# Cross-attention queries projected in the first output projection's stage and read back from DRAM, with the weighting of the values one step later

## What is computed

```
x1 = x + attention(layernorm(x)) @ o_proj.T          # first output projection
n  = layernorm(x1)
q  = rope(rms_norm(n @ Wq.T))        # 16 heads of 128; a head's norm is over its 128 columns
k  = rope(rms_norm(concat(ctx, n) @ Wk.T))           # 4 key heads, each for 4 query heads
v  = concat(ctx, n) @ Wv.T
x2 = x1 + (softmax(q k.T / sqrt(128)) v) @ Wo.T      # second output projection
```

## Time and profile before

| | |
|---|---|
| time, median of 3 runs | 2584.07 us (2581.47 to 2589.3) |
| profiled execution, span from the first to the last instruction | 2582.5 us |
| span of the first output projection (571 to 779) | 208 us |
| cross-attention before its first score (779 to 857.3) | 78.3 us |
| cross-attention, 60 steps with projections (857.3 to 1964.75) | 1107.45 us |
| cross-attention, last 4 steps and store (1964.75 to 2034) | 69.25 us |
| mean granted TensorE clock | 0.940 of full |

### The profile page before, as it was taken

How to read it: one execution, slowest core, us unless ns; L and a number is a source line. 1 busy time by engine, 2 the same in 40 slices (tenths; PEclk the granted TensorE clock), 3 DMA queues, 4 the chain that set the end, 5 groups by cost and what they waited for, 6 DMA issues and landing times. The chain is left out here.

```text
span 2582.5 us, 35584 instructions
## 1 busy us (share of the span) xinstructions
PE 2250.8 (87%) x10576; PEld 1665.7 (64%) x10576; DVE 1444.7 (56%) x3200; ACT 1022.2 (40%) x1998; POOL 784.9 (30%) x832
## 2 busy tenths in 40 slices
PE   5689999968975999999999999999998698928991
PEld 3578888857754666666666666666664476727771
DVE  3535555558764556565656565665664455535554
ACT  2323333334223444444454445444444422115660
POOL 1400000004553333333333333332331012136664
PEclk8899999989997999999999999999999899959996
DMA  7521221127764101111111011111100443235335
GB/s 274 164 72 36 65 64 32 37 73 230 223 190 166 37 12 45 40 44 40 44 41 44 12 44 41 44 40 44 40 15 15 147 111 92 63 120 189 110 102 191
DMA packets 229859, 218.95 MB, mean 85 GB/s; under 512 B 113394, under 2 KB 191714, under 8 KB 227298
## 3 DMA queue, kind: packets, MB, share of 16 engines
q1 hardware_dynamic: 212770, 180.46, 22.3%
q0 software_dynamic: 6496, 18.37, 2.6%
q10 hardware_dynamic: 10464, 18.77, 2.1%
HBM read 136.72 MB, written 80.83 MB: 84 GB/s over the span
## 5 line engine op out<-in xcount | busy, mean ns | idle before, releaser
L1820 DVE TENSOR_REDUCE ca_top<-ca_ps_s 112x1 f32<-112x487 f32 x256 | 169.3, 661 | 353.7 <-PE ca_ps_s L1608 351.6
L1708 ACT ACTIVATE ca_prob<-ca_ps_s,ca_down,ca_q_scale 112x487 f32<-112x487 f32 x256 | 193.9, 758 | 194.9 <-DVE ca_down L1822 194.8
L1608 PE MATMUL ca_ps_s<-ca_kT,ca_qT 128*112 128x487 f32 x512 | 241.0, 572 | 0.8 <-ACT ca_kT L1694 0.8
L1523 POOL TENSOR_TENSOR ca_q_scale<-ca_ssum,ca_minus_half 112x4 f32<-112x4 f32 x64 | 64.5, 1007 | 571.4 <-DVE ca_ssum L1809 571.4
L1626 PE MATMUL ca_ps_o<-ca_pT,ca_v 125*128 125x448 f32 (+1 forms) x512 | 222.4, 559 | 2.5 <-ACT ca_pT L1715 2.5
L91 PE MATMUL out_ps_y<-out_w_hi,out_o_hi 128*128 128x512 f32 x448 | 185.1, 413 | 33.2 <-DVE out_o_lo L1174 32.8
L1615 PEld LDWEIGHTS ca_ps_t<-ca_ident,ca_prob 112*125 112x125 f32 x1024 | 140.7, 188 | 109.2 <-DVE ca_prob L1829 76.7
L91 PE MATMUL ca_ps_p<-ca_w_hi,ca_xh 128*112 128x512 f32 x384 | 184.1, 479 | 29.2 <-DMA ca_tab<-rope_tables 25.2
L1615 PE MATMUL ca_ps_t<-ca_ident,ca_prob 112*125 112x112 f32 x1024 | 164.8, 283 | 42.3 <-DVE ca_prob L1829 42.2
L93 PE MATMUL out_ps_y<-out_w_hi,out_o_lo 128*128 128x512 f32 x448 | 180.5, 403 | 0.0
L92 PE MATMUL out_ps_y<-out_w_lo,out_o_hi 128*128 128x512 f32 x448 | 180.3, 403 | 0.0
(11 more groups left out here) (271 smaller groups left out, 5457.8 us busy)
## 6 DMA issues: line engine op xcount, KB each, us to landing
self_outT<-sa_ov SPq DMA_DIRECT2D x64, 224.0 KB, 2.4
out_o_raw<-self_outT SPq DMA_DIRECT2D x56, 256.0 KB, 4.2
cross_outT<-ca_ov SPq DMA_DIRECT2D x64, 224.0 KB, 2.3
out_o_raw<-cross_outT SPq DMA_DIRECT2D x56, 256.0 KB, 3.3
ffn_raw<-in_expert_w SPq DMA_DIRECT2D x8, 1536.0 KB
ca_c_raw<-in_ctxT SPq DMA_DIRECT2D x16, 750.0 KB, 6.4
expert_rows<-ffn_yt ACTq DMA_DIRECT2D x42, 256.0 KB, 2.0
rope_tables<-out_tab SPq DMA_DIRECT2D x16, 640.0 KB, 4.2
```

The costliest lines, as they stand in the source:

```text
L1608: pe.matmul(ps_s[j % 2][:, :], qT[:, i, j, :], kT[par][:, i, :], start=True, stop=True).then_inc(scored.sem, 1)
L1708: act.activation(prob[j][:, 0:KV], ps_s[j % 2][:, :], ACT.Exp, bias=down[:, j:j + 1], scale=q_scale[par][:, i, j:j + 1], accum_out=total[: ...
L1820: dve.tensor_reduce(top[:, j:j + 1], ps_s[j % 2][:, :], AX.X, ALU.max, negate=True).then_inc(maxed.sem, 1)
```

## The change

The queries leave the cross-attention. `self_output` takes the place of `project_out` in the first output stage, keeps all of its work and does more in each tile: it projects the queries of the tile it has just turned (`query`, four units of 12 matmuls), ACT squares them, DVE multiplies them with a table and sums the squares (`rotate`), POOL adds, roots and scales them (`unit`), PE turns them (`turn_q`), ACT copies them (`keep`) and SP stores them in DRAM as `cross_qT`. 14 tiles of 128 rows take the place of 16 sequences of 112 rows. The query weights (4 MB) are loaded and split here, their `lo` parts by POOL. The raw loads share memory with the `lo` parts (`both`), so a chunk of the next tile is loaded only when PE has used this one (`used`). The guest's `angles`, `sine` and `make` work on 128 x 320 elements, for the tables of the 128-row tile.

The cross-attention loads one 224 KB piece of `cross_qT` in each step, splits two weights and not six, and its `step` has another order: `weigh` of the step before stands behind the first two scores, the two projections follow, and DVE's sums of squares are set apart from `rotate`. The scale and the `down` product are gone. `cross_output` is the old `project_out` with its router branch alone.

```diff
+            def rotate(t, i, par):
...
+                if i == 0:
+                    wait(dve, guest.made, t)
+                wait(dve, q_sq, t, i)
+                wait(dve, q_turned, t, i - 2)
+                dve.tensor_tensor(h4(r1), h4(ps), over_heads(tab[:, 4, 0, :], HQ), ALU.mult)
+                for half in range(2):
+                    this, other = slice(half * HF, (half + 1) * HF), slice((1 - half) * HF, (2 - half) * HF)
+                    ins = dve.tensor_tensor(h4(r2)[:, :, this], h4(ps)[:, :, other],
+                                            over_heads(tab[:, 4, 1, this], HQ), ALU.mult)
+                ins.then_inc(q_rot.sem, 1)
+                wait(dve, q_rooted, t, i - 2)
+                dve.tensor_reduce(sm, h4(sq[i % 2][:, :]), AX.X, ALU.add).then_inc(q_sum.sem, 1)
+                wait(dve, q_sum, t, 2 * i)
+                f = 1.0 / X_SCALE ** 2
+                dve.tensor_scalar(sm, sm, f / HD, RMS_EPS * f, ALU.mult, ALU.add).then_inc(q_sum.sem, 1)
...
+            def body(t, h, par, ahead=True, last=False):
+                turn(t, par)
+                if ahead:
+                    low(t + 2, 0)
+                    low(t + 2, 1)
+                if not last:
+                    add(t + 1, h + par, 1 - par)
+                rotate(t, 0, par)
+                if not last:
+                    scale(t + 1, 1 - par)
+                if ahead:
+                    low(t + 2, 2)
+                rotate(t, 1, par)
+                if ahead:
+                    low(t + 2, 3)
+                guest.angles(dve, t + 2, par)
+                rotate(t, 2, par)
+                rotate(t, 3, par)
...
+            def unit(t, i):
+                a, b, par = q1[i % 2][:, :], q2[i % 2][:, :], i % 2
+                wait(pool, q_rot, t, i)
+                pool.tensor_tensor(a, a, b, ALU.add).then_inc(q_added.sem, 1)
+                wait(pool, q_sum, t, 2 * i + 1)
+                pool.tensor_tensor(rstd[par][:, :], ssum[par][:, :], minus_half[:, :], ALU.pow).then_inc(q_rooted.sem, 1)
+                wait(pool, q_rooted, t, i)
+                wait(pool, q_added, t, i)
+                heads = a.rearrange("p (h d) -> p h d", h=HQ)
+                pool.tensor_tensor(heads, heads, along(rstd[par][:, :], HD), ALU.mult).then_inc(q_ready.sem, 1)
...
+            def body(t, h, par, last=False):
+                if not last:
+                    layer.root(pool, t + 1, minus_half)
+                for i in range(NQ):
+                    unit(t, i)
+                guest.make(pool, t + 2, h + 1, par)
...
+            def body(t, h, par, ahead=True, first=False):
+                if not first:
+                    keep(t - 1, 2)
+                    keep(t - 1, 3)
+                turn(t, h, par)
+                if ahead:
+                    high(t + 2, 0)
+                    high(t + 2, 1)
+                square(t, 0)
+                if ahead:
+                    high(t + 2, 2)
+                square(t, 1)
+                if ahead:
+                    high(t + 2, 3)
+                guest.sine(act, t + 2, par)
+                square(t, 2)
+                keep(t, 0)
+                square(t, 3)
+                keep(t, 1)
...
+            def query(t, i, par):
...
+                wait(pe, q_rot, t, i - 2)
...
+            def turn_q(t, i):
+                wait(pe, q_ready, t, i)
+                wait(pe, q_kept, t, i - 2)
...
+            def body(t, par, first=False, last=False):
+                if not last:
+                    project(t + 1, 1 - par, 0)
+                if not first:
+                    turn_q(t - 1, 2)
+                if not last:
+                    project(t + 1, 1 - par, 1)
+                if not first:
+                    turn_q(t - 1, 3)
+                turn(t, par)
+                if not last:
+                    project(t + 1, 1 - par, 2)
+                    project(t + 1, 1 - par, 3)
+                query(t, 0, par)
+                query(t, 1, par)
+                query(t, 2, par)
+                turn_q(t, 0)
+                query(t, 3, par)
+                turn_q(t, 1)
```

The order of the new query work on ACT, DVE, PE and POOL is that of the four `body` functions above. In the cross-attention PE's and DVE's lists change so:

```diff
+            def step(b, h, i, par, more):
+                score(b, h, i, 0, par)
+                score(b, h, i, 1, par)
+                if begun(b, i):
+                    pb, pi = before(b, i)
+                    weigh(pb, pi, par if i else 1 - par)
                 if more:
-                    project(b + 1, i, 0, 1 - par)
+                    keys(b + 1, h + par, i, 1 - par)
                 turn(b, i, 0)
-                score(b, i, 2, par)
                 turn(b, i, 1)
-                score(b, i, 3, par)
+                score(b, h, i, 2, par)
+                score(b, h, i, 3, par)
                 if more:
-                    project(b + 1, i, 1, 1 - par)
-                    turn_q(b + 1, i)
+                    values(b + 1, i, 1 - par)
                 turn(b, i, 2)
                 turn(b, i, 3)
                 if more:
-                    project(b + 1, i, 2, 1 - par)
-                weigh(b, i, par, (0, 1))
-                if more:
                     turn_k(b + 1, i)
-                weigh(b, i, par, (2, 3))
 
             batches(pe, start, step)
+            weigh(B - 1, 3, 1)
...
+            def step(b, h, i, par, more):
+                maximum(b, i, 0)
+                maximum(b, i, 1)
                 divide(b, i, 0)
                 divide(b, i, 1)
                 if more:
-                    rotate(b + 1, i, 0, 1 - par)
-                maximum(b, i, 2, par)
-                maximum(b, i, 3, par)
+                    rotate(b + 1, h + par, i, 1 - par)
+                maximum(b, i, 2)
+                maximum(b, i, 3)
+                if more:
+                    squares(b + 1, i)
                 divide(b, i, 2)
                 divide(b, i, 3)
-                if more:
-                    rotate(b + 1, i, 1, 1 - par)
-
```

More of the change, by code:

```diff
@@ new lines, in _ @@
+            for h in range(H):
+                sp.dma_start(w_raw[:, h, :], w_src[:, h, :]).then_inc(w_in[h // HQ], 16)
+                if h % HQ == 0:
+                    load(0, h // HQ)
+                if h == 0:
+                    guest.load(sp)
+            residual(0, 0)
+            residual(1, 1)
+            for c in range(NQ):
+                sp.dma_start(wq_raw[:, c, :, :], wq_src[:, :, c * D:(c + 1) * D]).then_inc(wq_in[c], 16)
+                load(1, c)
+            body(0, 0, 0, first=True)
@@ new lines, in _ @@
+            body(1, 0, 1)
+            with sp.Fori(1, TT // 2 - 1) as h:
+                for par in range(2):
+                    body(h * 2 + par, h, par)
+            for par in range(2):
+                body(TT - 2 + par, TT // 2 - 1, par, ahead=False)
+            store_q(TT - 1, 2)
+            store_q(TT - 1, 3)
+            for par in range(2):
+                guest.store(sp, TT + par, par)
+            for par in range(2):
+                sp.wait_ge(guest.put[par].sem, guest.put[par].at(B // 2 - 1))
+                sp.wait_ge(y_put[par].sem, y_put[par].at(TT // 2 - 1))
+                sp.wait_ge(x_put[par].sem, x_put[par].at(TT // 2 - 1, 1))
+                sp.wait_ge(q_put[par].sem, q_put[par].at(TT - 1, 1))
@@ L1249, in body @@
                     low(t + 2, 1)
-                if rope is not None:
-                    guest.angles(dve, t + 2, par)
-                if router is not None and not (isinstance(t, int) and t < 2):
+                if not (isinstance(t, int) and t < 2):
                     locate(t - 2, par)
@@ L1500, in _ @@
-            for b in (B - 2, B - 1):
-                for i in range(4):
-                    store(b, i)
+                    body(h * 2 + par, h, par, more=2)
+            body(B - 2, B // 2 - 1, 0, more=1)
+            body(B - 1, B // 2 - 1, 1, more=0)
+            store(B - 1, 3)
             for i in range(2):
@@ L1581, in project @@
                 for k in range(KD):
[L1582 removed]
+                    mm = mm3(pe, ps_p[0][0:m, :], a_hi[:, k, :], a_lo[:, k, :], w_hi[:, 0, k, :], w_lo[:, 0, k, :],
                              k == 0, k == KD - 1)
[L1584 to L1592 removed]
+                mm.then_inc(k_mm.sem, 1)
@@ L1594, in turn_k, with values @@
+            def values(b, i, par):
+                if first(b) and i == 0:
+                    pe.wait_ge(w_lo_ready, 2)
+                m, a_hi, a_lo = operands(b, i, par)
+                wait(pe, v_ready, b, i - 1)
+                for k in range(KD):
+                    mm = mm3(pe, ps_p[1][0:m, :], a_hi[:, k, :], a_lo[:, k, :], w_hi[:, 1, k, :], w_lo[:, 1, k, :],
+                             k == 0, k == KD - 1)
+                mm.then_inc(v_mm.sem, 1)
             def turn_k(b, i):
```

941 lines of the change are left out of this document (544 added, 397 removed).

## The result

The changed kernel takes 2627.92 us (median of 4 runs, 2624.09 to 2631.26), the kernel before 2586.69 us (median of 4, 2581.47 to 2590.89). The ratio is 1.0159, with a 95% interval from 1.0139 to 1.0178: 41 us slower, where 82 were forecast (2666 us).

The account below looks back on a forecast made before the run. PE was taken to bound the attention steps, and a loop through PE, ACT, DVE and POOL the new output stage. 2582.5 + 294 - 177 - 23 - 12, with 1.6 to the median, gave 2666 us; range 2575 to 2715.

Parts of the forecast that it names:

- The output stage: First output stage: a loop through PE, ACT, DVE and POOL of 28.6 us a tile, 32.2 with waits; +294 us.
- the term of 3.6: Output-stage tile: small scalings, norm's scaling, two splits and two angle operations held up by POOL, 3.6 us in all.
- the rival on the clock: Output-stage tiles: TensorE's clock falls in the pauses, 2.4 us a tile or 31 us, giving 2697 us; chance 14%.
- The first turn: Output stage's first turn: later than 605.24 through 4 MB more loads and splits; at 620, between 612 and 625.
- The attention's start: Attention ahead of the first score: fewer weight splits and projections, 55 us in place of 78.3; -23 us.
- The attention step: 60 attention steps: 15.5 us each in place of 18.46, with divides waiting for POOL; -177 us.
- divides constant at 0.47: Attention steps: a sign of a wrong forecast, that divides keep 0.47 us and don't wait for POOL.
- The second rival: Output tile as forecast, but the attention's divide doesn't wait for POOL: step 14.65 us, time 2615 us; chance 13%.
- The end: Last 4 attention steps: `weigh` of the step before covers the softmax, 3.0 us in each; -12 us.
- The rest: Second output stage and experts: no change, 0 us.

Follow-up runs that it names:

- The two moves: Changed kernel with chunk 1 and the tile's turn ahead of `turn_q(t - 1, 2)`: 2572.19 us; separately, with the guest's angles and sines behind the last query unit: 2557.03 us.
- the experiment with the useless add: Changed kernel with a second POOL add of 125 x 512 to an unused buffer and DVE's sums of squares behind the last two divides: 2820.78 us.
- the second pair: The kernel before and the changed kernel, each profiled once more without edits: 2588.34 and 2630.46 us.

## Why the prediction was right, and where it was not

The direction, the ways and the range were right, though the rise was half the 82 us forecast. By its own steps:

- **The output stage** was forecast as a loop of 28.6 us and 3.6 of waits for POOL; 32.2 against 32.46 measured, +294 against +297.7. The two moves show that it is this loop: each breaks it at another place, and the tile falls to 27.6 and 26.9. That the sum is so close is partly luck: within it two terms were off and cancelled. From `rotate` 0 to the end of the angles it took 10.8 us (858.46 to 869.27), 1.9 more than the 8.9 of undisturbed work: the term of 3.6 was too large, since it counted POOL's root among the operations that hold DVE up. And from `turn_q(t - 1, 2)` to the turn it took 5.0 and 6.0 by turns in place of 3.9, because TensorE's clock had fallen in the wait; the rival on the clock had the mechanism and 2.4 us for it, and the forecast had nothing. From the turn to `rotate` 0 it was 9.7 against 9.3, POOL's chain 4.99 against 4.9, ACT's part 1.38 against 1.5.
- **The first turn** came at 618.4 against 620, between 613.5 and 624.3 in the other profiles with POOL's splits.
- **The attention's start** gave the 23 us that were forecast.
- **The attention step** is the step that failed: "The first then ends with the root at 13.05, the second with POOL's scaling at 14.35". Up to there the chain held (squares' small scaling until 11.66 against 11.65, root from 11.73 against 11.7). Then the root held nobody up, both divides were through at 12.84, and POOL's scaling began 0.11 behind them. The step is 14.80 in the mean and not 15.5: 42 us, and the forecast was 38 too high. Of the signs that the prediction set down for being wrong, "divides constant at 0.47" is the one that came. The assumption under the failed step, that the divide stands still where it meets POOL, holds for POOL's large operations: beside an add it takes 1.03. The second rival was nearer in size (14.65, 2615), with a reason that was wrong: a divide that never waits.
- **The end** gave 18.8 us, not 12: without `weigh` as cover PE not only waits, it also works partly at the lower clock (0.84 granted in the kernel before, 0.80 with `weigh` in its own step, 0.99 in the changed kernel).
- **The rest** was taken as unchanged; it added 8.9 in this pair of profiles and 1.8 in the second pair.

The Trainium skill, "SBUF — State Buffer", "Who interferes with whom", was weighed for the divide, and the trace agrees with it in part: a float32 scaling is a form that competes (1.03 us beside an add, in the experiment with the useless add). The Trainium skill says there that the lock is held "for the whole instruction"; the root of 125 x 4 lasted 1.14 us and held up neither of two divides that ran inside it, so for that operation the measurement decides against it.

What stays open: how long within POOL's root the memory is in use at all, and what sets the last stages' scatter of 14 us.

## What to carry to other kernels

When work moves into a loop whose engines have fixed lists, add up the longest way round the loop through all engines; here 13 us of new PE work a tile cost 20, and moving lines without removing an instruction got 84 us back. A wait of 4 us on PE costs more than itself, since the granted clock was lower behind it (0.92 in such a stage, 1.00 without the waits). Before a wait for a shared resource is put into a sum, ask for each operation on the other side whether it is large: the 125 x 512 add held DVE up, the 125 x 4 root, equally long, did not.
